# Windowed attention from the third step on: masks and turned blocks in halves of 64 rows

## The reference, cut to what matters

```python
bq = bq * jnp.cos(qf) * qs + _rotate_half(bq) * jnp.sin(qf) * qs
bk = bk * jnp.cos(freqs) * inv_s + _rotate_half(bk) * jnp.sin(freqs) * inv_s
sim = jnp.einsum('bwie,bwje->bwij', bq, bk)
mask = (bq_k[:, None, :] - ws > b_t[:, :, None]) | (b_t[:, :, None] > bq_k[:, None, :] + ws) | pad_mask[:, None, :]
sim = jnp.where(mask[None], NEG, sim)
attn = jax.nn.softmax(sim, axis=-1)
out = jnp.einsum('bwij,bwje->bwie', attn, bv)
return out @ w_out.T
```

## Time and profile before

| what | us |
|---|---|
| median of three runs | 982.56 |
| the profiled execution, its own time | 981.5 |
| its span | 980.2 |
| TensorE busy | 953.6 (97%) |
| TensorE weight loads busy | 634.2 (65%) |
| VectorE busy | 665.7 (68%) |
| ScalarE busy | 505.8 (52%) |
| GpSimd busy | 434.9 (44%) |
| granted TensorE clock | full, in all 40 slices |

### The profile page before, as it was taken

The page is one execution under the profiler, slowest core; times in us unless marked ns, Lnnn a source line. Parts: engine busy times, 40 slices in busy tenths (PEclk is TensorE's granted clock), DMA queues, the critical chain, the costliest instruction groups (busy, mean ns, idle before and its releaser), DMA issues.

```text
span 980.2 us, 13545 instructions
## 1 busy us (share of the span) xinstructions
PE 953.6 (97%) x4508; PEld 634.2 (65%) x4508; DVE 665.7 (68%) x1577; ACT 505.8 (52%) x1164; POOL 434.9 (44%) x343
## 2 busy tenths in 40 slices
PE   5899999999999999999999999999999999999998
PEld 3565666676657766676666766667666676657655
DVE  5957769587675876667775778748777487625823
ACT  3574783636746276452754537545474535645222
POOL 5858247551185402763047520665108541056343
PEclk9999999999999999999999999999999999999999
DMA  7060240613423034230532205332153313433061
GB/s 282 11 175 1 35 130 0 143 44 11 132 68 97 22 31 121 80 97 1 85 81 86 76 2 97 90 76 65 1 112 76 86 44 9 134 85 90 1 163 33
DMA packets 63237, 72.80 MB, mean 74 GB/s; under 512 B 33272, under 2 KB 34040, under 8 KB 62784
## 3 DMA queue, kind: packets, MB, share of 16 engines
q1 hardware_dynamic: 61744, 69.94, 30.8%
q10 hardware_dynamic: 1424, 2.00, 0.7%
HBM read 69.04 MB, written 2.88 MB: 73 GB/s over the span
## 4 chain that ended last, share of the span: by engine, by line
PE 88%; DVE 7%; issue 2%; ACT 2%; DMA 0%; POOL 0%; DVEq 0%; ACTq 0%; POOLq 0%
PE ps L633 12%; PE ps L740 12%; PE ps L488 9%; PE ps L490 9%; PE ps L489 9%; PE ps L542 6%; PE ps L555 6%; PE ps L569 5%; PE ps L641 3%; PE ps L715 2%; PE ps L483 1%; PE ps L523 1%; PE ps L533 1%; PE ps L704 1%; PE ps L513 1%
## 5 line engine op out<-in xcount | busy, mean ns | idle before, releaser
L1143 ACT ACTIVATE wide<-ps 128x512 f32<-128x512 f32 x136 | 81.0, 596 | 211.4 <-PE ps L490 210.9
L1069 ACT ACTIVATE pw<-ps,w_cols 128x512 f32<-128x512 f32 x144 | 98.6, 688 | 98.4 <-PE ps L490 97.0
L1030 ACT ACTIVATE pw<-ps,nmax 128x256 f32<-128x256 f32 x256 | 117.8, 474 | 50.3 <-DVE nmax L1391 45.8
L1870 POOL TENSOR_TENSOR atc<-atc,wide 128x512 f32<-128x512 f32 x64 | 82.2, 1284 | 125.4 <-DVE atc L1605 125.4
L633 PE MATMUL ps<-pw,w_w 128*128 128x512 f32 x288 | 135.4, 592 | 0.0
L1850 POOL TENSOR_TENSOR kr<-qks,w_rope 128x512 f32<-128x512 f32 x32 | 43.8, 1368 | 157.4 <-DVE qks L1369 157.4
L1407 DVE COPY pt<-ps 128x512 f32<-128x512 f32 x126 | 81.6, 678 | 26.2 <-PE ps L555 25.9
L488 PE MATMUL ps<-yc,eg 128*128 128x512 f32 x128 | 94.3, 737 | 0.0
L1870 POOL TENSOR_TENSOR pt<-pt,wide 128x512 f32<-128x512 f32 x48 | 61.7, 1286 | 64.6 <-DVE pt L1605 63.5
L1391 DVE TENSOR_REDUCE nmax<-ps 128x4 f32<-128x1024 f32 (+1 forms) x80 | 79.0, 1004 | 13.4 <-PE ps L542 13.4
L633 PEld LDWEIGHTS ps<-pw,w_w 128*128 128x128 f32 x288 | 53.5, 189 | 42.6 <-issue 37.8
(11 more groups left out here) (225 smaller groups left out, 2132.7 us busy)
## 6 DMA issues: line engine op xcount, KB each, us to landing
wb<-scratch SPq DMA_DIRECT2D x128, 256.0 KB, 4.0
wb<-scratch SPq DMA_DIRECT2D x32, 512.0 KB, 5.7
wide<-scratch SPq DMA_DIRECT2D x16, 512.0 KB, 5.8
xin<-in_x SPq DMA_DIRECT2D x8, 256.0 KB, 2.9
out<-wide SPq DMA_DIRECT2D x8, 256.0 KB
wb<-in_w SPq DMA_DIRECT2D x1, 1152.0 KB, 8.8
w_w<-in_w SPq DMA_DIRECT2D x1, 1152.0 KB, 12.3
w_ed<-in_ed SPq DMA_DIRECT2D x1, 1024.0 KB, 15.8
```

The lines of the kernel that those rows point to most:

```text
L1030: m = act.activation(pw[:, u % 2, j, :], ps[:, score_bank(u, par), qt * SEQ:(qt + 1) * SEQ], ACT.Exp, bias=nmax[:, u % 3, j:j + 1], scale= ...
L1069: act.activation(hid[:, n % 4, :], bank(UPS0[n % 2]), ACT.Gelu, bias=cols[:, C_B1 + 2 * e + c:C_B1 + 2 * e + c + 1], scale=1.0).then_inc(* ...
L1870: pool.tensor_tensor(hh[h], hh[h], sgl[:, (c + 1) % 3, :], ALU.mult).then_inc(*HH_POOL.one)
```

## The change

1. Masks. `mask` and `short_ident` get a second layout, in which each half of 64 rows holds what the other half held. `scores` now lays each bank's mask with two products of 64 rows each, par 0 in the upper and par 1 in the lower half of the array, in all steps. It takes both banks first and waits for `MASKS`, which GpSimd sets after eight small selections at the start; ScalarE writes the second identity with two more activations.
2. Turned blocks. From step 2 on, units 1 to 6 are turned by `turn_by_halves`: sixteen transposes of 64 rows by 128 columns instead of eight of 128 by 128. Rows 0 to 63 of all eight blocks go to bank 0 and rows 64 to 127 to bank 7, in turn. It waits for both exponentials and both banks first, and one update at the end releases both copies. `pt_copy_half` copies a bank into every second stretch of 64 columns of `pt`. Units 0 and 7 are turned as before.
3. Order of TensorE from step 2 on. Both turns of unit 0 and the output rows now stand ahead of the scores of unit 2; the scores of units 3 and 4 stand ahead of the turns of units 1 and 2; the expert half E0,0 stands ahead of the values of pair 2.

The start of the stage on TensorE, before: unit 0's two turns (L555), the output rows (L656), the scores of unit 2 (L533, L542), then unit 1's first turn and unit 3's scores.

```diff
@@ -140,8 +140,8 @@
         eu = sb("eu", [P, 2, CH1, P], F32R)
 
         ident = sb("ident", [P, P])
-        short_ident = sb("short_ident", [P, P], BF16)
-        mask = sb("mask", [P, 2, P], BF16)
+        short_ident = sb("short_ident", [P, 2, P], BF16)
+        mask = sb("mask", [P, 2, 2, P], BF16)
         half_power = sb("half_power", [P, 2, TILES])
 
         x1 = sb("x1", [P, TILES, D])
@@ -272,7 +272,8 @@
         WB = [semaphore(f"wb{k}") for k in range(RING)]
         STAGED = [semaphore(f"staged{k}") for k in range(2)]
 
-        CONSTANTS, IDENT, SHORT_IDENT = event("constants"), event("ident"), event("short_ident")
+        CONSTANTS, IDENT, SHORT_IDENT = event("constants"), event("ident"), event("short_ident", 2)
+        MASKS = event("masks")
         VARIANCE, RSTD = [event("variance0"), event("variance1")], [event("rstd0"), event("rstd1")]
         SHIFT = [event("shift0"), event("shift1")]
         Y0_ROWS, Z0_ROWS, Y1_ROWS, Z1_ROWS = (event(n) for n in ("y0_rows", "z0_rows", "y1_rows", "z1_rows"))
@@ -525,14 +526,22 @@
                           start=False, stop=True).then_inc(*VALUES.one)
                 freed[k] = VALUE_ROWS.at(s, t)
 
+            def half_rows(h):
+                return slice(64 * h, 64 * h + 64)
+
             def scores(s, u):
                 p, g = u // G, u % G
                 banks = [score_bank(u, par) for par in range(2)]
                 for b in banks:
                     take(b)
-                    pe.matmul(ps[:, b, P:3 * P], short_ident[:, :],
-                              mask[:, :, :].rearrange("p q k -> p (q k)"), start=True, stop=False,
-                              skip_group_check=True)
+                w.wait_ge(*MASKS.at(0))
+
+                for h in range(2):
+                    for par, b in enumerate(banks):
+                        rows = half_rows(par)
+                        pe.matmul(ps[:, b, P:3 * P], short_ident[rows, h, :],
+                                  mask[rows, h, :, :].rearrange("p q k -> p (q k)"), start=h == 0, stop=False,
+                                  skip_group_check=True)
                 w.wait_ge(*ROPED_K.at(s, p))
                 w.wait_ge(*ROPED.at(s, p))
                 for qt in range(2):
@@ -556,6 +565,21 @@
                                      pw[:, u % 2, 2 * par + qt, kt * P:(kt + 1) * P], ident[:, :])
                 m.then_inc(*TRANSPOSED.one)
                 freed[k] = PT.at(s, 2 * u + par)
+
+            def turn_by_halves(s, u):
+
+                for par, k in enumerate(TURN_BANKS):
+                    w.wait_ge(*EXPS.at(s, 2 * u + par))
+                    take(k)
+                for j in range(8):
+                    par, kt, qt = j // 4, j // 2 % 2, j % 2
+                    for h, k in enumerate(TURN_BANKS):
+                        m = pe.transpose(bank(k)[:, j * 64:j * 64 + 64],
+                                         pw[half_rows(h), u % 2, 2 * par + qt, kt * P:(kt + 1) * P],
+                                         ident[half_rows(h), half_rows(h)])
+                m.then_inc(TRANSPOSED.sem, 2)
+                for h, k in enumerate(TURN_BANKS):
+                    freed[k] = PT.at(s, 2 * u + h)
 
             def weigh(s, u):
 
@@ -754,22 +778,34 @@
                     scores(s, 0)
                     logits0(0, 6)
                     scores(s, 1)
-                for u in range(UNITS):
+                if s > 1:
+                    turn(s, 0, 0)
+                    turn(s, 0, 1)
+                    rows1(s - 2, 1)
+                    scores(s, 2)
+                    for u in range(1, UNITS - 1):
+                        if u > 1 and u % G == 1:
+                            weigh_pair(s, u // G - 1)
+                        if u < 3:
+                            scores(s, u + 2)
+                        turn_by_halves(s, u)
+                        if 2 < u < UNITS - 2:
+                            scores(s, u + 2)
+                    up0_half(s, E0, 0)
+                    weigh_pair(s, PAIRS - 2)
+                    turn(s, 7, 0)
+                    turn(s, 7, 1)
+                    up0_half(s, E0, 1)
+                for u in range(UNITS if s < 2 else 0):
                     if u > 1 and second:
                         weigh(s, u - 1)
-                    if s > 1 and u > 1 and u % G == 1:
-                        weigh_pair(s, u // G - 1)
                     turn(s, u, 0)
                     if u and first or u == 1 and second:
                         weigh(s, u - 1)
                     if u == 0 and second:
                         rows0(0, VALUE_BANK)
-                    if u < 3 and s > 1:
-                        scores(s, u + 2)
                     turn(s, u, 1)
-                    if u == 0 and s > 1:
-                        rows1(s - 2, 1)
-                    if u < UNITS - 2 and (u > 2 or s < 2):
+                    if u < UNITS - 2:
                         scores(s, u + 2)
                     if u == 5 and first:
                         turn_weights0(s, score_bank(5, 1))
@@ -780,9 +816,9 @@
                     if u == 6 and second:
                         uv(0, 0, 1, 4)
                         v1(0, 0, 5)
-                    if u == 6 and not second:
+                    if u == 6 and first:
                         up0_half(s, E0, 0)
-                    if u == 7 and not second:
+                    if u == 7 and first:
                         up0_half(s, E0, 1)
                 if second:
                     v1(0, 1, 2)
@@ -1282,7 +1318,11 @@
                 lay1(x)
 
             w.wait_ge(*IDENT.at(0))
-            act.activation(short_ident[:, :], ident[:, :], ACT.Identity).then_inc(*SHORT_IDENT.one)
+
+            act.activation(short_ident[:, 0, :], ident[:, :], ACT.Identity)
+            for h in range(2):
+                act.activation(short_ident[:, 1, (1 - h) * 64:(1 - h) * 64 + 64], ident[:, h * 64:h * 64 + 64],
+                               ACT.Identity).then_inc(*SHORT_IDENT.one)
             z0_rows(0)
             y0_rows(0)
             z0_cols(0, 6)
@@ -1407,6 +1447,14 @@
                 dve.tensor_copy(pt_of(u)[:, 4 * par:4 * par + 4, :].rearrange("p a q -> p (a q)"),
                                 bank(TURN_BANKS[par])).then_inc(*PT.one)
 
+            def pt_copy_half(s, u, h):
+
+                w.wait_ge(*TRANSPOSED.at(s, 2 * u + 1))
+                if u >= 3:
+                    w.wait_ge(*WEIGHED.at(s, u - 3))
+                dve.tensor_copy(pt_of(u)[:, :, 64 * h:64 * h + 64],
+                                bank(TURN_BANKS[h]).rearrange("p (a q) -> p a q", q=64)).then_inc(*PT.one)
+
             def invert(s, u):
                 p, g = u // G, u % G
                 w.wait_ge(*EXPS.at(s, 2 * u + 1))
@@ -1620,10 +1668,11 @@
                     rope_out(s, 1, 3)
                     rope_in(s, 3, 1)
                 for u in range(UNITS):
-                    pt_copy(s, u, 0)
+                    copied = pt_copy_half if s > 1 and 0 < u < UNITS - 1 else pt_copy
+                    copied(s, u, 0)
                     if u == 0 and s > 1:
                         maxima(s, 2)
-                    pt_copy(s, u, 1)
+                    copied(s, u, 1)
                     if u == 0 and second:
                         x1_rows(0, VALUE_BANK)
                     if u == 1 and s > 1:
@@ -1830,12 +1879,28 @@
                 pool.affine_select(out=ident[:, :], in_=ident[:, :], compare_op=ALU.not_equal, fill=1.0,
                                    base=0, pattern=[[-1, P]], channel_multiplier=1).then_inc(*IDENT.one)
                 pool.memset(half_power[:, :, :], -0.5)
-                own(pool.memset(mask[:, :, :], 0.0))
+                own(pool.memset(mask[:, :, :, :], 0.0))
                 for qt, sign in enumerate((1, -1)):
-                    m = pool.affine_select(out=mask[:, qt, :], in_=mask[:, qt, :], compare_op=ALU.is_ge,
+                    m = pool.affine_select(out=mask[:, 0, qt, :], in_=mask[:, 0, qt, :], compare_op=ALU.is_ge,
                                            fill=MASKED, base=0, pattern=[[-sign, P]],
                                            channel_multiplier=sign)
                 m.then_inc(*CONSTANTS.one)
+
+            def masks_further_on():
+
+
...
+                m.then_inc(*MASKS.one)
 
             def power(layer, s):
                 w.wait_ge(*VARIANCE[layer].at(s))
@@ -2026,6 +2091,7 @@
             constants()
             power(0, 0)
             split_wv()
+            masks_further_on()
             rope_turn(0, 0)
             rope_turn(0, 1)
             w.wait_ge(*HIGH.at(0))
```

More of the change, by code:

```diff
@@ L1838, in constants @@
                 m.then_inc(*CONSTANTS.one)
+            def masks_further_on():
+                for qt, sign in enumerate((1, -1)):
+                    for b in range(2):
+                        part = mask[:, 1, qt, b * 64:b * 64 + 64]
+                        own(pool.affine_select(out=part, in_=part, compare_op=ALU.is_ge, fill=MASKED,
```

(8 more changed lines are left out.)

## The result

The change makes the kernel slower: 997.26 us (median of six runs, 996.18 to 999.54) against 983.40 of the kernel before on the same chip. The ratio is 1.0141, with a 95% interval of 1.0123 to 1.0159. The profiled execution took 996.18 us with a span of 994.9, so it is 14.7 over the span of before. The forecast was 983.0 with a range of 973 to 992.

The account below looks back on a forecast made before the run. TensorE, busy for 97% of the span, was taken as the bound, with VectorE and ScalarE close behind. The profiled 981.5 us, plus 6 x 0.5 for the stages, minus 1.5 outside them, gave 983.0; range 973 to 992.

Parts of the forecast that it names:

- Pairs at 0.06: Turns of units 1 to 6: each side-by-side pair of half transposes takes 0.06 us, 0.48 a unit against 0.87.
- the rival of halves in turn: Half transposes take turns, a pair at 0.109 us or more: 991 us; chance 0.21 shared with masks in turn and dearer copies.
- Copies 0.60 apart: Copies out of PSUM in rows of 64 are priced as today's, 0.60 us apart.
- Masks in halves pass side by side: Scores blocks: four mask instructions run in two side-by-side pairs, 0.22 us as now; 0.44 if they take turns.
- The gain outside the stages, 1.5: 28 scores blocks outside the six stages save 0.07 us each, 2.0, less 0.5 in step 0: 1.5 us.
- The output rows wait for ScalarE's lay: Stage start: after eight transposes end at 0.87 us, output rows wait until 0.94; unit 2's scores start at 1.75, maxima 2.83.
- Steps 2 to 5: Rest of the stage, units 1 to 7: waits for copies and exponentials make it end at 28.0 us, 0.5 late.
- The 4.0 us of saved work and 4.7 of waits: Each of six stages: TensorE has 4.0 us less to do, but waits of some 4.7 swallow it and 0.5 more.
- The third rival: Saved work arrives because copies, maxima and exponentials keep up, decided at unit 3: 956 us, half of it 968; chance 0.14.

Follow-up runs that it names:

- the run with the weights by rows: The changed kernel with layer-0 weights sent to DRAM as 128 rows of 128 bytes, not 4096 pieces of 4 bytes, from the second step: 990.10 us.
- the mixed order: The kernel before with masks in halves, turns by halves in units 3, 4, 5, 7, some scores and maxima earlier, layer-0 weights turned on VectorE: 969.21 us.
- the old start: The changed kernel with unit 2's scores put back between unit 0's two turns, halves kept: 1001.38 us, ratio 1.0181.

## Why the prediction was wrong

Taken by its steps, for the part of TensorE first.

- *Pairs at 0.06*: 0.065, right; the rival of halves in turn is refuted. Copies 0.60 apart: right. Masks in halves pass side by side: L542 x4 takes 0.39, and the stage alone gains 0.36. The gain outside the stages, 1.5: 1.3 in the profiled execution.
- *"The output rows wait for ScalarE's lay"* (step 1 of its table) is the step that failed first. The second turn of unit 0 writes bank 7, which the layer-1 experts have just filled and `lay1` empties. The order printed ahead of the prediction even names that wait (s_lay1) on the turn, and I put it on the rows of output behind it. Four transposes, 0.5 us, thus moved behind the wait: the scores of unit 2 start at 2.26 (1.75 foretold), its maxima at 3.34 (2.83), unit 1's turn at 5.37 (4.80). Before, the same wait cost nothing, since the scores of unit 2 stood in front of it.
- *Steps 2 to 5* then keep their form and add delay. In undisturbed stages (the run with the weights by rows) unit 3 is turned at 11.37 (10.59 foretold), unit 4 at 13.76 (12.99), the values of pair 1 start at 15.49 (14.70), unit 6 is turned at 20.16 (19.2). The stage ends at 29.0, not 28.0: 1.54 late instead of 0.5. Six times the missing 1.0 is 6 us. Of this 1.0 the misplaced wait is 0.51; the rest are hand-overs priced some hundredths short, each on the path: the delay against the table is 0.65 at the maxima of unit 3, 0.78 at its turn and 0.96 at unit 6's. That is read from the timelines; no run takes out the wait for `lay1` alone. Moving the scores of unit 2 back takes out 1.51, which is this wait and the part of the move that was foretold.
- *The 4.0 us of saved work and 4.7 of waits.* The trace has 4.6 of waits in such a stage (0.43 for `lay1`, then 1.00, 0.39, 1.22, 0.59 and 1.00) and 3.1 less busy time. Busy time counts the tail of the last instruction before each wait; from start to start the six gaps sum to 6.8, and without the waits they would be some 1.3 (an estimate: 0.11 each between instructions, and 0.2 more where the tile shape changes). That makes the waits 5.5, not 4.7, and with the stage 1.54 longer leaves the saved work near 4.0, as foretold.
- *No term for the pieces.* This is the second step that failed: the prediction read no row of DMA at all and put the pieces at nothing. The stages lose 6.8 us more in the profiled execution, and 7.8 in the medians. It carries the time from 989, where the steps above end, to the measured 997.
- *The rivals.* None was right. "The halves take turns" gave 991 and the right sign for a wrong reason. The third rival, saved work that arrives, was refused by the written order and is what the mixed order does, at 969.2 us, half of the priced gain; its place (unit 3) was named rightly.
- *The range* took in errors of a price. It held none for a step placed wrongly in the order, and none for a resource that costs the kernel before nothing.

So 983.0 + 6.2 (six times 1.04, the wait for `lay1` and the hand-overs behind it) + 6.8 to 7.8 (pieces) is 996 to 997. What stays open is how a backlog of small writes reaches TensorE. Shown is what appears with it: its signals come up to 2 us and more late, it stands amid a block with nothing to wait for, fetches of instructions take four times as long. Long fetches as the one carrier are excluded by the runs above. Whether signals and instructions share a path with the pieces was not shown, nor why the same program loses 0 in one stage and 2 in the next, nor why the old start, with less waiting in it, loses nearly three times as much to the pieces as the new one.

## What to carry to other kernels

When a change puts a step in front of another, list for each of its instructions the bank it writes and who empties that bank last, and start the count of delays there. When saved work on the bound engine comes from tying two results together, move the neighbour's input (here the scores and maxima of the unit after next) ahead of the tie, and tie only where both results are there anyway. Look for transfers in pieces of 4 bytes before making an engine issue denser: this kernel carried them for nothing until it did, and one 0.21 us transpose on VectorE removed them (the Trainium skill, "VectorE: DVE Perf Modes", section The three transpose paths, limits it to blocks of 32x32, which 32 weights a token just fill).

## What the runs showed of the hardware

- Two 64-row transposes of 64 columns each, with 128 columns of weights, pass side by side in 0.065 us, 0.033 an instruction. The Trainium skill, "TensorE: Matmul & The Clock Gate", section "Wait — 56ns, not 53.3ns?", gives 62 ns per matmul for a TensorE whose instructions are not decoded in hardware; this case is below it.
- 4096 pieces of 4 bytes to DRAM took 35.9% of 16 DMA engines for 9 us and left them at 53.4%, for 0.26 MB, in the next 8; 1024 pieces cost no stage more than 0.1 us (29.01 to 29.10).
- Signals from TensorE to VectorE, otherwise followed within 0.1 us, came some 2 us late beside such a backlog. The same pieces cost 0 us (full turns, the order of before), 2.2 (full turns, mixed order), 7.8 (this change), 11.5 (halves, mixed order) and 21.2 (this change with the old start, with the lower clock in it).
- During a pause of TensorE of 4.55 us the granted clock fell from 1.00 to 0.50, and the sixteen instructions of the values behind it took 3.68 us instead of 1.95.
- A 16 KB fetch of instructions beside the pieces took 3.6 to 6.2 us in the changed kernel, otherwise mostly 0.9 to 1.5; in the kernel before one of 4.5 us cost its stage nothing (27.48).
